# Second attention layer: reciprocals turned as 16 columns and spread to 128 rows by two DMA transfers

## The chip, the cores and the metric

One core of one Trainium2 chip runs one program. The metric is the device time of one execution in microseconds (us); smaller is better. The engines are named as the profile names them: PE is TensorE's matrix unit (PEld its weight loads), DVE is VectorE, ACT is ScalarE, POOL is GpSimd, and SP is the sync engine, which here only issues DMA transfers. The core's transfers run on 16 DMA engines.

## The reference

Two attention layers follow one another over 16 graphs of 512 tokens and 384 features (12 heads of 32). Cut to what matters here:

```python
h = maximum(layernorm(x), 0)
x = x + L0(h, adj, ...)          # scores/sqrt(32) + beta*adj, masked where adj == 0
h = maximum(layernorm(x), 0)
# L1:
scores = einsum('bqhd,bkhd->bhqk', q, k) * scale + bias      # bias = adj + adj
row_nonzero = any(scores != 0, axis=-1, keepdims=True)
p = nan_to_num(softmax(where(row_nonzero, scores, -inf)))
out = einsum('bhqk,bkhd->bqhd', p, v).reshape(b, n, h)
x = x + out @ Wo.T + bo
```

In layer 1 every row (a token of a head) of the output has to be multiplied by the reciprocal of its softmax sum, or by zero where the whole row of scores is zero. The kernel does it after the product with v and before the product with Wo.

## The kernel before

There are 32 graph passes, `g`, 16 for each layer. A pass has three chunks, `c`; a chunk is four heads (128 features). A chunk has four steps, `t`, one for each tile of 128 queries. So a pass has 12 steps, numbered 0 to 11, and the text says "step 6 of a pass". A chunk's work runs on long after its own four steps: what it does at place 14.50, counted from step 0 of its pass, falls into step 2 of the next pass.

In a step PE computes the scores of the following tile (L248). DVE adds the bias and takes the minimum (L393) and transposes the tile before in 32x32 blocks (`turn`, L406). ACT takes the four exponentials (`exp`, L516). PE also has a list of other items in each step. The table `PLACES` says where each stands: `hT` turns of the next pass's input, `qk` and `v` projections, `sums` and `zero` for the test of zero rows, `tp` turns of the chunk's last tile of probabilities, `pv` the product with v in three parts, `spread` the reciprocals, and `post` the product with Wo. All of them except `pv` write to a ring of three PSUM banks. An item may start only when the item three places ahead of it in the ring has been copied out by ACT or DVE.

Each engine runs its instructions strictly in the order of the code. On ACT, an item that PE issued in a step is normally copied in the middle of the next step's exponentials. The function `soon_of` makes an exception: everything up to the last `spread`, `tp`, `turn` or `hT` of a step's list is copied directly behind that same step's four exponentials.

SP issues `move(g, c)`, 16 transfers of 192 KB between two SBUF tensors, `pk<-pt`, in two halves of eight. The first half waits for three turned tiles of the chunk and for the `pv` of the chunk before, the second half for one more part of that `pv`. `pv` part 1 of the chunk needs the first half landed, part 2 the second. The reciprocals go this way: DVE `recip`, POOL `keep` (the mask, then a product that writes 128x512 numbers, each reciprocal repeated over the 32 columns of its head), PE `spread` (four transpositions of 128x128, L300), ACT a copy of 128x512 into `rspread`, which shares its memory with `mask` and shows under that name (L586), and DVE `scale_out` (L444), which multiplies the finished `pv` of the chunk and releases `pv_done`. `pv` part 0 of the next chunk and `post` wait for `pv_done`.

Of the kernel before, what the change touches and what calls it, by code (L numbers as in the profile page):

```python
# [6 lines left out]
F32 = mybir.dt.float32  # L7
F32R = mybir.dt.float32r
ACT = mybir.ActivationFunctionType
ALU = mybir.AluOpType  # L10
# [32 lines left out]
def chunk(s):  # L43

    return s // DT, s % DT
# [15 lines left out]
    "zero": (2.53, 6.40, 10.40),  # L61
    "tp": (3.31, 3.32, 3.33, 3.34, 7.31, 7.32, 7.33, 7.34, 11.31, 11.32, 11.33, 11.34),
    "pv": (5.20, 6.70, 8.32, 9.20, 10.70, 12.32, 13.20, 14.70, 16.32),
    "spread": (7.30, 12.30, 16.61),
    "post": (17.50, 17.60, 18.50, 20.50),
})

# [58 lines left out]
SPLITS = {(B - 1, 1, 1): 2, (B - 1, 1, 3): 0, (B - 1, 2, 1): 1}  # L126


def two_layers(nc, x, adj, weights, bq, bk, bv, bo, beta, x1, out, mem):

    scale = float(HD) ** -0.5, float(D) ** -0.5

# [6 lines left out]
    with ExitStack() as ctx:  # L139
        def sem(name):  # L140
            return ctx.enter_context(nc.semaphore(name))
# [12 lines left out]
        recip_dve, recip_done, keep_step, ksum_done = sem("recip_dve"), sem("recip_done"), sem("keep_step"), sem("ksum_done")  # L154
        v_added, biassum_done, part_done = sem("v_added"), sem("biassum_done"), sem("part_done")
        stats_done, mv_done, rstd_step, h_done = sem("stats_done"), sem("mv_done"), sem("rstd_step"), sem("h_done")
        hT_high, mask_done, bias_done = sem("hT_high"), sem("mask_done"), sem("bias_done")
        scaled, res_added, bo_added = sem("scaled"), sem("res_added"), sem("bo_added")
        last_stored = sem("last_stored")
# [5 lines left out]
        def nth(kind, g, i):  # L165
            return per_graph[kind] * (g - B if kind in ("sums", "zero", "spread") else g) + i + 1
# [17 lines left out]
        @block.sync  # L184
        def _(sp):
            def load_weight(layer, n):
                sp.dma_start(m.raw[layer][n], weights[layer][n].rearrange("(t p) n -> p t n", p=P)).then_inc(raw_in[layer][n], 16)

            def load_row(dst, row, signal):
                sp.dma_start(dst[:], row.rearrange("(a n) -> a n", a=1).to_broadcast([P, D])).then_inc(signal, 16)  # L190

            def move(g, c):

                s = DT * g + c
                if s == LAST:
                    return
                sp.wait_ge(turned, TURNS * (s + 1))
                for half in range(HALVES):
                    if s:
                        sp.wait_ge(pv_ready, PARTS * (s - 1) + half + 2)  # L200
                    for n in range(QUADS):
                        for a in (half, half + HALVES):
                            to = (a - half + n) % QUADS
                            sp.dma_start(m.pk[HD * to:HD * (to + 1), a], m.pt[HD * a:HD * (a + 1), s % 2, to]).then_inc(moved[layer_of(g)][c][half], 16)  # L204

            sp.dma_start(m.xin[:], tokens(x[0])).then_inc(x_first, 16)
            load_weight(0, 0)
            load_weight(0, 1)
            sp.dma_start(m.beta[:], beta.rearrange("(a n) -> a n", a=1).to_broadcast([P, 1])).then_inc(small_in, 16)
            sp.dma_start(m.bq[:], bq).then_inc(small_in, 16)  # L210
            sp.dma_start(m.bk[:], bk).then_inc(small_in, 16)
            load_weight(0, 2)
            load_row(m.bva, bv[0], bv_in[0])
            load_row(m.bvx, bv[1], bv_in[1])
            for g in range(GRAPHS):
                for c in range(STEPS):
                    move(g, c)

                    if (g, c) == (B - 2, 2):
                        load_weight(1, 2)  # L220
                    if (g, c) == (B - 1, 0):
                        for n, last in ((0, 2), (1, 0)):
                            sp.wait_ge(weights_split[last], 2)
                            load_weight(1, n)
                        sp.wait_ge(v_added, NT * B)
                        load_row(m.bva, bo, bo_in)
                    if (g, c) == (B, 1):
                        sp.wait_ge(res_added, NT * B)
                        sp.dma_start(m.wo[:], weights[1][3].rearrange("(t p) n -> p t n", p=P)).then_inc(wo_in, 16)
            for i in range(NT):  # L230
                sp.wait_ge(done["post"], nth("post", GRAPHS - 1, i))
                sp.dma_start(tokens(out[B - 1])[:, i], m.res[:, i, :]).then_inc(last_stored, 16)
            sp.wait_ge(last_stored, 16 * NT)

        @block.tensor
        def _(pe):
# [14 lines left out]
            def item(kind, g, i):  # L251
# [44 lines left out]
                    mm = nc.tensor.transpose(to[:, 0:P], m.headsum[:], m.ident[:])  # L296
                if kind == "spread":
                    pe.wait_ge(recip_done, nth("spread", g, i))
                    for t in range(NT):
                        mm = nc.tensor.transpose(to[:, P * t:P * (t + 1)], m.rwide[:, t, :], m.ident[:])  # L300
                if kind == "post":
                    if i == 0:
                        pe.wait_ge(pv_done, DT * (g + 1))
# [67 lines left out]
        def _(dve):  # L371
# [66 lines left out]
            def scale_out(g, c):  # L438

                if c == 0:  # L440
                    dve.wait_ge(ready["post"], nth("post", g - 1, NT - 1))
                dve.wait_ge(done["spread"], nth("spread", g, c))
                dve.wait_ge(pv_ready, PARTS * (DT * g + c + 1))
                nc.vector.tensor_tensor(m.oT[:, c, :], m.out[:], m.rspread[:], ALU.mult).then_inc(pv_done, 1)  # L444

# [63 lines left out]
        def _(act):  # L509
# [21 lines left out]
            def item(kind, g, i):  # L531
# [47 lines left out]
                    nc.scalar.activation(m.v[:, g % 2, i, :], frm[:, 0:D], ACT.Copy).then_inc(done["v"], 1)  # L579
                if kind == "spread":  # L580
                    act.wait_ge(ready["spread"], nth("spread", g, i))
                    if g == B and i == 0:
                        act.wait_ge(bias_done, NT * B)
                    else:
                        act.wait_ge(pv_done, DT * g + i)
                    nc.scalar.activation(m.rspread[:], frm, ACT.Copy).then_inc(done["spread"], 1)  # L586

            def soon_of(g, c, t):

# [42 lines left out]
        def _(pool):  # L632
# [98 lines left out]
            def keep(g, c):  # L731
# [16 lines left out]

                def wide(ap):
                    return ap.rearrange("p t (j o) -> p t j o", o=1).to_broadcast([P, NT, HC, HD])  # L750
                nc.gpsimd.tensor_tensor(m.rwide[:].rearrange("p t (j e) -> p t j e", e=HD), wide(m.recip[g % 2][:, :, HC * c:HC * (c + 1)]),
                                        wide(m.mz[:]), ALU.mult).then_inc(recip_done, 1)

# [73 lines left out]
class Memory:  # L827
    def __init__(self, nc, ctx):
        def sb(name, shape, dt=F32):
            return ctx.enter_context(nc.sbuf_tensor(name, shape, dt))  # L830
# [34 lines left out]
        self.mz, self.rz = sb("mz", [P, NT, HC]), sb("rz", [P, NT, HC])  # L865
        self.recip = [sb(f"recip{i}", [P, NT, H]) for i in range(2)]
        self.ksum1, self.ksum = sb("ksum1", [P, 2]), sb("ksum", [P, 2, HD])
        self.headsum = sb("headsum", [P, P])
        self.oT = sb("oT", [P, DT, N])
        self.onorm = self.wo  # L870
# [4 lines left out]

def two_attention_layers(nc: bass.Bass, x, adj, wq0, bq0, wk0, bk0, wv0, bv0, beta0, wq1, wk1, wv1, bv1, wo1, bo1, out):
    x1 = nc.dram_tensor("x_between", [B, N, D], F32, kind="Internal").ap()
    with ExitStack() as ctx:
        mem = Memory(nc, ctx)
        two_layers(nc, x, adj, ((wq0, wk0, wv0), (wq1, wk1, wv1, wo1)), bq0, bk0, (bv0, bv1), bo1, beta0, x1, out, mem)  # L880


# [29 lines left out]
```

## Time and profile before

| | us |
|---|---|
| median of 3 runs | 1988.66 (1985.5 to 1992.04) |
| the profiled execution | 1990.03 |
| its span | 1988.3 |
| PE busy | 1900.5 (96%) |
| DVE busy | 1828.6 (92%) |
| ACT busy | 1676.5 (84%) |
| POOL busy | 913.0 (46%) |
| mean share of the 16 DMA engines, queue of SP | 63.3% |
| the same, queue of POOL | 18.4% |

The profiled execution took 1.4 us more than the median of the runs. The span is the part of it that the trace covers. Layer 1 takes up the second half, from about 975 us on. Busy shares are averages over both layers; a share under 100% can still hide an engine that is the limit in one stage.

### The profile page before, as it was taken

The numbers are of one execution on the slowest core, as the hardware profiler recorded it, in microseconds if no ns is written. First come the engines' busy times: TensorE is split into PE (matmuls) and PEld (weight loads), VectorE is DVE, ScalarE is ACT, GpSimd is POOL, SyncE is SP. The second block draws the span as 40 slices with busy tenths as digits, with TensorE's granted clock in tenths as the row PEclk, the third lists the DMA queues.
The fourth block names the chain that finished last, engine by engine and source line by source line (L and its number), as shares of the span: only waits on it lengthen the run. The fifth ranks groups of instructions, "written<-read, shape, count | busy, mean of one in ns | idle before, by whom it ended". The sixth has DMA issues, their size and how long they took to land.

```text
span 1988.3 us, 50014 instructions
## 1 busy us (share of the span) xinstructions
PE 1900.5 (96%) x18336; PEld 1229.1 (62%) x18336; DVE 1828.6 (92%) x3989; ACT 1676.5 (84%) x4275; POOL 913.0 (46%) x1114
## 2 busy tenths in 40 slices
PE   5999999999999999997999999999999999999998
PEld 3566666666666666664666666666666666666665
DVE  5999999999999999997989999999999999999984
ACT  4999999999999999997977887887887888887885
POOL 5465556556655455561353334343343334343331
PEclk9999999999999999998999999999999999999999
DMA  3888999988899898889787788778787788777884
GB/s 134 197 215 220 228 225 234 229 228 223 230 226 230 231 233 226 226 224 225 201 218 198 187 215 222 189 202 210 193 216 194 189 221 211 199 200 202 203 200 113
DMA packets 104723, 415.92 MB, mean 209 GB/s; under 512 B 27008, under 2 KB 31104, under 8 KB 104480
## 3 DMA queue, kind: packets, MB, share of 16 engines
q1 hardware_dynamic: 77728, 305.24, 63.3%
q0 software_dynamic: 26752, 107.49, 18.4%
q8 instruction: 147, 2.41, 0.5%
q14 instruction: 96, 0.79, 0.1%
HBM read 88.61 MB, written 25.17 MB: 57 GB/s over the span
## 4 chain that ended last, share of the span: by engine, by line
PE 49%; DVE 25%; ACT 11%; DMA 6%; SPq 5%; issue 3%; POOL 1%; DVEq 0%; POOLq 0%
DVE s L393 13%; PE sc L248 11%; PE ring L281 11%; DVE pt L406 10%; PE out L340 9%; PE ring L309 6%; ACT s L516 6%; SPq L204 5%; PE ring L265 5%; PE ring L288 4%; DMA pk<-pt 4%; ACT xin L523 2%; PE ring L274 2%; ACT pl L548 1%; PE ring L300 1%
## 5 line engine op out<-in xcount | busy, mean ns | idle before, releaser
L516 ACT ACTIVATE s<-s,nmax 128x512 f32<-128x512 f32 x1536 | 1094.9, 726 | 157.6 <-DVE nmax L393 157.5
L393 DVE CUSTOM_DVE_ANT_0 s<-sc,bias 128x512 f32<-128x512 f32 x1536 | 968.0, 686 | 53.0 <-PE sc L248 25.2
L406 DVE STREAM_TRANSPOSE pt<-s 128x2048 f32<-128x2048 f32 x285 | 656.8, 2304 | 0.0
L248 PE MATMUL sc<-k,q 32*128 32x512 f32 x3072 | 439.9, 642 | 51.0 <-DVE nmax L393 36.2
L516 ACT ACTIVATION_READ_ACCUMULATOR s<-s,nmax 128x1 f32 x1536 | 311.0, 202 | 0.0
L340 PE MATMUL out<-pk,v 128*32 128x192 f32 x6080 | 287.2, 330 | 6.0 <-DMA pk<-pt 6.0
L340 PEld LDWEIGHTS out<-pk,v 128*32 128x32 f32 x6080 | 178.8, 110 | 140.4 <-issue 87.4
L288 PE MATMUL ring<-wv,hT 128*128 128x384 f32 x1152 | 236.3, 349 | 0.0
L281 PE MATMUL ring<-hT,wq 128*128 128x512 f32 x864 | 228.1, 409 | 1.5 <-DVE hT L421 1.5
L281 PE MATMUL ring<-hT,wk 128*128 128x512 f32 x864 | 228.0, 408 | 0.0
L248 PEld LDWEIGHTS sc<-k,q 32*128 32x128 f32 x3072 | 121.5, 184 | 164.0 <-DVE nmax L393 82.8
L281 PEld LDWEIGHTS ring<-hT,wk 128*128 128x128 f32 x864 | 156.3, 190 | 102.1 <-issue 72.0
L548 ACT ACTIVATE pl<-ring 128x512 f32<-128x512 f32 x384 | 198.0, 604 | 24.0 <-PE ring L265 24.0
L265 PEld LDWEIGHTS ring<-ident,s 128*128 128x128 f32 x1536 | 165.7, 141 | 77.2 <-issue 51.6
L281 PEld LDWEIGHTS ring<-hT,wq 128*128 128x128 f32 x864 | 156.4, 190 | 85.2 <-issue 52.5
L288 PEld LDWEIGHTS ring<-wv,hT 128*128 128x128 f32 x1152 | 195.7, 188 | 21.5 <-issue 17.0
L265 PE MATMUL ring<-ident,s 128*128 128x128 f32 x1536 | 196.2, 279 | 6.2 <-ACT pl L548 5.7
L686 POOL TENSOR_TENSOR v<-v,bvx 128x384 f32<-128x384 f32 x64 | 64.5, 1007 | 295.0 <-ACT v L579 295.0
L686 POOL TENSOR_TENSOR v<-v,bva 128x384 f32<-128x384 f32 x64 | 64.6, 1010 | 262.4 <-ACT v L579 262.3
L393 DVE DVE_READ_ACCUMULATOR2_ANT nmax<- 128x1 f32 x1536 | 127.5, 83 | 0.0
L309 PE MATMUL ring<-wo,oT 128*128 128x384 f32 x360 | 126.6, 495 | 0.0
L675 POOL TENSOR_SCALAR mask<-bias 128x512 f32<-128x512 f32 x64 | 123.3, 1927 | 1.3 <-DMA bias<-in_adj 0.6
(93 smaller groups left out, 1891.4 us busy)
## 6 DMA issues: line engine op xcount, KB each, us to landing
pk<-pt SPq DMA_DIRECT2D x1520, 192.0 KB, 4.9
bias<-in_adj POOLq DMA_DIRECT2D x32, 1024.0 KB, 10.3
res<-in_x POOLq DMA_DIRECT2D x16, 768.0 KB, 7.4
x_between<-res POOLq DMA_DIRECT2D x16, 768.0 KB, 4.5
xin<-x_between POOLq DMA_DIRECT2D x16, 768.0 KB, 10.1
res<-x_between POOLq DMA_DIRECT2D x16, 768.0 KB, 10.6
xin<-in_x POOLq DMA_DIRECT2D x15, 768.0 KB, 9.8
out_x<-res POOLq DMA_DIRECT2D x15, 768.0 KB, 7.0
```

The lines of the kernel that those rows point to most:

```text
L248: mm = nc.tensor.matmul(m.sc[:, j, :], m.q[rows, s % 2, P * t:P * (t + 1)], m.k[rows, s % 2, :], start=True, stop=True)
L265: mm = nc.tensor.transpose(to[:, P * n:P * (n + 1)], m.s[:, TURNS % 2, j, P * n:P * (n + 1)], m.ident[:])
L281: mm = nc.tensor.matmul(to, w[y][:, t, P * a:P * (a + 1)], m.hT[x][:, t, :], start=n == 0, stop=n == 3 * DT - 1)
L288: mm = nc.tensor.matmul(to[:, 0:D], m.hT[x][:, t, P * i:P * (i + 1)], m.wv[y][:, t, :], start=n == 0, stop=n == 3 * DT - 1)
L309: mm = nc.tensor.matmul(to[:, 0:D], o, m.wo[:, t, :], start=t == 0, stop=t == DT - 1)
L340: mm = nc.tensor.matmul(to, v[:, n, P * c + HD * j:P * c + HD * (j + 1)], p, start=n == 0, stop=n == QUADS - 1)
L393: nc.vector.tensor_tensor_reduce(out=m.s[:, t % 2, j, :], in0=m.sc[:, j, :], in1=m.bias[g % 2][:, t, :], scale=s_scale[layer], scalar=3.0e ...
L406: nc.vector.transpose(out=to, in_=m.s[:, t % 2].rearrange("p j (i a e) -> p (j i) a e", a=QUADS, e=HD)).then_inc(turned, 1)
L516: nc.scalar.activation(tile, tile, ACT.Exp, bias=m.nmax[s % 2][:, t, j:j + 1], scale=-1.0, accum_out=m.sums[s % 2][:, t, j:j + 1]).then_in ...
L548: nc.scalar.activation(m.pl[:, j, :], frm, ACT.Copy).then_inc(done["tp"], 1)
L675: nc.gpsimd.tensor_scalar(m.mask[:], tile, 0.0, masked, ALU.is_le, ALU.mult).then_inc(mask_done, 1)
L686: nc.gpsimd.tensor_tensor(v, v, (m.bva, m.bvx)[layer_of(g)][:], ALU.add).then_inc(v_added, 1)
```

## The change

Of the 48 chunks of layer 1, 47 change; the last keeps the old way. POOL now writes only 16 columns (`rcols`: four heads times four tiles). PE turns them in one transposition into 16 rows of 128. ACT copies those 16x128 numbers into `rrows`. SP then stores them to DRAM, waits until they have landed, waits for the `scale_out` of the chunk before, and loads them back, each head's row of 512 numbers repeated over 32 partitions, into `rspread`. DVE waits for that transfer instead of for ACT. The places of `spread` move from 7.30, 12.30 and 16.61 to 6.50, 10.50 and 14.50.

```diff
-    "spread": (7.30, 12.30, 16.61),
+    "spread": (6.50, 10.50, 14.50),
...
+            def spread_rows(g, c):
+
+                s = DT * g + c
+                n = s - DT * B
+                sp.wait_ge(done["spread"], nth("spread", g, c))
+                if n > 1:
+                    sp.wait_ge(spread_in, 16 * (n - 1))
+                sp.dma_start(rows[n % 2].rearrange("(r e) -> r e", e=P), m.rrows[:]).then_inc(rows_stored, 16)
+                sp.wait_ge(rows_stored, 16 * (n + 1))
+                if n:
+                    sp.wait_ge(pv_done, s)
+                else:
+                    sp.wait_ge(bias_done, NT * B)
+                sp.dma_start(m.rspread[:], rows[n % 2].rearrange("(j o n) -> j o n", j=HC, o=1).to_broadcast([HC, HD, N])).then_inc(spread_in, 16)
...
                 for c in range(STEPS):
+                    if DT * g + c > DT * B:
+                        spread_rows(*chunk(DT * g + c - 1))
                     move(g, c)
...
                     pe.wait_ge(recip_done, nth("spread", g, i))
-                    for t in range(NT):
-                        mm = nc.tensor.transpose(to[:, P * t:P * (t + 1)], m.rwide[:, t, :], m.ident[:])
+                    if DT * g + i == LAST:
+                        for t in range(NT):
+                            mm = nc.tensor.transpose(to[:, P * t:P * (t + 1)], m.rwide[:, t, :], m.ident[:])
+                    else:
+                        mm = nc.tensor.transpose(to[0:NT * HC, 0:P], m.rcols[:], m.ident[:])
...
-                dve.wait_ge(done["spread"], nth("spread", g, c))
+                if DT * g + c == LAST:
+                    dve.wait_ge(done["spread"], nth("spread", g, c))
+                else:
+                    dve.wait_ge(spread_in, 16 * nth("spread", g, c))
...
-                    if g == B and i == 0:
-                        act.wait_ge(bias_done, NT * B)
+                    if DT * g + i == LAST:
+                        act.wait_ge(pv_done, LAST)
+                        nc.scalar.activation(m.rspread[:], frm, ACT.Copy).then_inc(done["spread"], 1)
                     else:
-                        act.wait_ge(pv_done, DT * g + i)
-                    nc.scalar.activation(m.rspread[:], frm, ACT.Copy).then_inc(done["spread"], 1)
+                        if (g, i) > (B, 0):
+                            act.wait_ge(rows_stored, 16 * (nth("spread", g, i) - 1))
+                        nc.scalar.activation(m.rrows[:], frm[0:NT * HC, 0:P], ACT.Copy).then_inc(done["spread"], 1)
...
+                if s < LAST:
+                    nc.gpsimd.tensor_tensor(m.rcols[:].rearrange("p (j t) -> p t j", t=NT), m.recip[g % 2][:, :, HC * c:HC * (c + 1)],
+                                            m.mz[:], ALU.mult).then_inc(recip_done, 1)
+                    return
```

On ACT, steps 5 to 9 of a steady pass of layer 1 stood so before. L516 are exponentials, L523 the next pass's input (`xin`), L566 the copy of `k`, L586 the spread copy, L548 the copies of `tp`, L551 those of `hT`:

```order
802 L516 ACTIVATE s,sums<-s,nmax 128x512 x4
803 L523 ACTIVATE xin<-xin,nmr,rstd 128x384 x2
804 L516 ACTIVATE s,sums<-s,nmax 128x512
805 L566 ACTIVATE k,ksum<-ring 128x512
806 L516 ACTIVATE s,sums<-s,nmax 128x512 x3
807 L586 ACTIVATE mask<-ring 128x512
808 L548 ACTIVATE pl<-ring 128x512 x4
809 L551 ACTIVATE hT<-ring 128x512 x3
```

Now the same place reads (the lines of the changed file are other ones, L590 is the copy of `k`, L612 the copy of the 16 rows):

```order
793 L540 ACTIVATE s,sums<-s,nmax 128x512 x4
794 L590 ACTIVATE k,ksum<-ring 128x512
795 L612 ACTIVATE rrows<-ring 16x128
796 L547 ACTIVATE xin<-xin,nmr,rstd 128x384 x2
797 L540 ACTIVATE s,sums<-s,nmax 128x512 x4
798 L572 ACTIVATE pl<-ring 128x512 x4
799 L575 ACTIVATE hT<-ring 128x512 x3
```

The copy of `k` and the spread copy have both moved ahead of all four exponentials of step 7 and ahead of the two `xin`. The same has happened to the copy of `k` in steps 10 and 2.

On SP, one chunk of a steady pass was one `move`:

```order
245 L204 DMA pk<-pt 32x1536 [waits pv_ready,turned]
246 L204 DMA pk<-pt 32x1536 x7
247 L204 DMA pk<-pt 32x1536 [waits pv_ready]
248 L204 DMA pk<-pt 32x1536 x7
```

Now the store of the 16 rows and the load that repeats them stand ahead of it, each with waits of its own:

```order
251 L200 DMA rows<-rrows 16x128 [waits spread_in,spread_done]
252 L206 DMA mask<-rows 128x1x512 [waits pv_done,rows_stored]
253 L220 DMA pk<-pt 32x1536 [waits pv_ready,turned]
254 L220 DMA pk<-pt 32x1536 x7
255 L220 DMA pk<-pt 32x1536 [waits pv_ready]
256 L220 DMA pk<-pt 32x1536 x7
```

All 18 transfers of a chunk go through SP's one queue, and the `move` of a chunk is issued only after the store of the chunk before has landed.

## Rows read from the trace of the kernel before

**Rows 1.** Windows of one pass: busy us by engine, clock, DMA share, GB/s
```profile
1300.00:1362.00 62.00, 61.60 (x595) 39.78 (x593) 58.02 (x125) 50.13 (x133) 22.87 (x34) 1.00 0.81 204
1284.00:1286.00 2.00, 2.00 (x39) 1.21 (x41) 1.97 (x9) 2.00 (x7) 0.36 (x1) 1.00 1.04 253
```

**Rows 2.** Chain that ended last, one pass: start us, us, what
```profile
1298.58 4.07 PE ring L309 x12
...
1308.06 1.44 PE out L340 x32
...
1310.56 0.59 PE ring L300 x4
...
1314.45 1.07 PE sc L248 x8
...
1328.81 0.11 PE ring L296
...
1333.36 1.68 PE ring L288 x9
...
1336.31 0.69 DVE s L393
...
1354.50 1.14 PE sc L248 x8
1355.64 1.44 PE out L340 x32
...
1361.05 1.01 PE out L340 x32
1362.06 1.49 PE ring L309 x4
```

**Rows 3.** Groups by line in layer 1: busy us, mean ns, idle before
```profile
L586 ACT ACTIVATE mask<-ring 128x512 f32<-128x512 f32 x47 | 28.3, 601 | 32.4 <-PE ring L300 32.4
...
L576 ACT ACTIVATE headsum<-ring 128x128 f32<-128x128 f32 x46 | 12.7, 275 | 16.0 <-PE ring L293 16.0
```

**Rows 4.** Timeline, steps 6 and 7 of a pass, ACT
```profile
1302.46 1.29 ACT L523 ACTIVATE xin<-xin,nmr,rstd 128x384 f32<-128x384 f32 x2
...
1308.94 0.71 ACT L516 ACTIVATE s<-s,nmax 128x512 f32<-128x512 f32 x1
...
1311.68 2.06 ACT L548 ACTIVATE pl<-ring 128x512 f32<-128x512 f32 x4
```

**Rows 5.** Timeline, end of the last chunk
```profile
1968.66 2.08 ACT L548 ACTIVATE pl<-ring 128x512 f32<-128x512 f32 x4
...
1969.33 0.66 PE L265 MATMUL ring<-ident,s 128*128 128x128 f32 x4 [0.47 <-ACT pl L548]
```

**Rows 6.** SP's moves of a chunk, first and last: ns each, starts; landing
```profile
L204 SPq DMA_DIRECT2D pk<-pt x2: 507/552/597, 1310.9 to 1311.5; - x2
...
L204 SPq DMA_DIRECT2D pk<-pt x1: 590/590/590, 1321.9 to 1321.9; - x1
...
DMA to landing us min/median/max: 9.3/9.3/9.3
```

**Rows 7.** The same for the next chunk, first three and last two issues
```profile
L204 SPq DMA_DIRECT2D pk<-pt x3: 507/590/592, 1332.2 to 1333.4; - x3
...
L204 SPq DMA_DIRECT2D pk<-pt x2: 590/626/663, 1343.8 to 1344.5; - x2
...
DMA to landing us min/median/max: 8.4/8.7/9.1
```

**Rows 8.** DMA issues: KB each, median us to landing
```profile
out_x<-res SPq DMA_DIRECT2D x4, 192.0 KB, 1.9
...
bva<-in_bo SPq DMA_DIRECT2D x1, 192.0 KB, 4.3
```

**Rows 9.** Timeline: the product with the reciprocals in the next pass
```profile
1358.55 0.69 DVE L444 TENSOR_TENSOR oT<-out,mask 128x512 f32<-128x512 f32 x1 [0.17 <-ACT mask L586]
```

**Rows 10.** Timeline, first pass of layer 1, PE
```profile
1029.06 2.30 PE L340 MATMUL out<-pk,v 128*32 128x192 f32 x32 [2.12 <-DMA pk<-pt]
```

More of the change, by code:

```diff
@@ L126, with two_layers @@
 SPLITS = {(B - 1, 1, 1): 2, (B - 1, 1, 3): 0, (B - 1, 2, 1): 1}
-def two_layers(nc, x, adj, weights, bq, bk, bv, bo, beta, x1, out, mem):
+def two_layers(nc, x, adj, weights, bq, bk, bv, bo, beta, x1, rows, out, mem):
     scale = float(HD) ** -0.5, float(D) ** -0.5
@@ L156, in two_layers @@
         stats_done, mv_done, rstd_step, h_done = sem("stats_done"), sem("mv_done"), sem("rstd_step"), sem("h_done")
+        rows_stored, spread_in = sem("rows_stored"), sem("spread_in")
         hT_high, mask_done, bias_done = sem("hT_high"), sem("mask_done"), sem("bias_done")
@@ L867, in __init__ @@
         self.ksum1, self.ksum = sb("ksum1", [P, 2]), sb("ksum", [P, 2, HD])
+        self.rcols, self.rrows = sb("rcols", [P, NT * HC]), sb("rrows", [NT * HC, P])
         self.headsum = sb("headsum", [P, P])
@@ L877, in two_attention_layers @@
     x1 = nc.dram_tensor("x_between", [B, N, D], F32, kind="Internal").ap()
+    rows = [nc.dram_tensor(f"rows_{i}", [HC * N], F32, kind="Internal").ap() for i in range(2)]
     with ExitStack() as ctx:
         mem = Memory(nc, ctx)
-        two_layers(nc, x, adj, ((wq0, wk0, wv0), (wq1, wk1, wv1, wo1)), bq0, bk0, (bv0, bv1), bo1, beta0, x1, out, mem)
+        two_layers(nc, x, adj, ((wq0, wk0, wv0), (wq1, wk1, wv1, wo1)), bq0, bk0, (bv0, bv1), bo1, beta0, x1, rows, out, mem)
 def kernel(x, adj, L0_gnn_Wq, L0_gnn_bq, L0_gnn_Wk, L0_gnn_bk, L0_gnn_Wv, L0_gnn_bv, L0_gnn_beta,
```

## Prediction

> **What bounds the kernel now.** I read the windows first. In a steady pass of layer 1, PE is busy 61.60 of 62 us and DVE 58.02, so PE has no slack and DVE little. ACT has 50.13. The DMA engines are at 0.81 [rows 1]. The chain of waits then gives the rhythm: the two `post` products stand at 1298.58 and at 1362.06, so a pass takes 63.5 us. Most of it is PE's, except the stretch from 1336.3 to 1354.5, which is DVE's: there, PE work can go and nothing is won [rows 2]. There are 15 such intervals between the 16 passes of layer 1. Last I read SP's own moves and their landings, since the change puts two more transfers into that queue and makes SP wait for one of them.
>
> **The change part by part.**
>
> *PE.* Four transpositions are 0.59 us on the chain. A single one (the `zero` item) is 0.11 [rows 2]. In a pass, the one for chunk 2 (place 4.61, just ahead of the chain's PE part) gives back 0.59, since its successor moves to step 2, into DVE's stretch. The one for chunk 0 would give 0.48. The one for chunk 1 stood in DVE's stretch and comes back as 0.11 in step 10. Alone that is 0.96 us a pass.
>
> *ACT.* The copy shrinks from 601 ns to about the 275 ns of a 128x128 copy, and its wait for PE, 32.4 us in all, goes [rows 3]. POOL's last product shrinks too, and POOL is off the path. But ACT's order takes something back. In step 6, ACT now copies `k` and the 16 rows before `xin` and before the exponentials of step 7. PE turns the 16 columns after the `post` of that step, which ends at 1308.06 [rows 2], so they are there at 1308.2. Then come 0.28 for the copy, 1.29 for two `xin` and four exponentials of 0.71, so the copies of `tp` begin at 1312.6 and not at 1311.68 [rows 3, 4]. The four of them take 2.06 [rows 4]. The last turn of `hT` needs the fourth copy gone from the ring, so it can start at 1314.7 and ends about 0.5 later, at 1315.1. PE went on at 1314.45 before [rows 2]. So chunk 0 costs 0.65 instead of giving 0.48. That PE does wait on such a copy is seen at the end of the last chunk: the first copy starts at 1968.66, the fourth turn at 1969.33, 0.67 later, with a wait of 0.47 [rows 5]. In step 10, `k` is ready at 1328.8 [rows 2]; 0.57 for its copy, 0.28 and four times 0.71 bring the copies of `tp` to 1332.55, the fourth turn starts 0.67 later and ends by 1333.7, where PE was free at 1333.36 before [rows 2]: 0.3. In step 2 the same delay falls into DVE's stretch and costs nothing by these rows. Sum on PE and ACT: -0.59 + 0.65 + 0.3 = +0.4 us a pass.
>
> *The two transfers.* The store is small. The quickest landing of SP's is 1.9 us [rows 8]; I take that for it and 0.6 for an issue [rows 6]. The load that repeats the rows is not in the trace. From below: it writes 256 KB, and at 204 GB/s with a share of 0.81 [rows 1] that is 1.05 us of all engines. From above: the nearest row is the load of one row of `bo` to 128 partitions, 192 KB in 4.3 us [rows 8]. Less the 1.9 of a quick landing, 2.4 us by the count of its 128 rows, 3.2 by bytes. I take 2.8, as this row repeats a source too.
>
> The Trainium skill speaks to this load ("DMA: Bandwidth & Descriptors", "Why a DMA increments its semaphore by 16 and not by 1"): the number of engines is the largest up to 16 that divides the slowest dimension of both access patterns. The source's is four heads, so four engines would carry it all. No transfer in this trace has such a shape. By that rule the load costs more than its bytes suggest, and the sum would be that of the third rival below; by the bytes alone it would be that of the first.
>
> *Where these transfers stand.* SP's queue is served in order as far as the rows show: the moves of chunk 1 start at 1310.9, the last is issued at 1321.9 and lands 9.3 later, at 1331.2 [rows 6]. Those of chunk 2 start at 1332.2, the last is issued at 1344.5 and lands 9.1 later, at 1353.6 [rows 7]. PE takes that data at 1355.64 [rows 2], only 2.0 later. Now follow a pass:
> - The load for chunk 0 is issued ahead of the moves of chunk 1: they start 0.6 later and carry 2.8 more, so they end at 1334.6.
> - The 16 rows of chunk 1 are copied by ACT at about 1329.7, plus 0.65 for step 7. Their store stands behind those moves and lands at 1334.8. Before that SP issues nothing.
> - Then the load for chunk 1 (0.6) and the moves of chunk 2: from 1335.4, not 1332.2. They end at 1353.6 + 3.2 + 2.8 = 1359.6.
> - The 16 rows of chunk 2 are ready in step 2 of the next pass, around 1349, with the engines full (share 1.04 at the same place of the pass before [rows 1]). Their store lands at 1359.8. The load for chunk 2 lands 1.9 + 2.8 later, at 1364.5.
> - DVE's product with it stood at 1358.55 [rows 9]. It now ends at 1365.2. `pv` part 0 (1361.05 before) and `post` wait for it: 1.01 and 4.07 later [rows 2] PE is at 1370.3, where it was at 1366.1. That is +4.2 us a pass.
>
> A second count, by the load of the queue: 0.81 of 63.5 is 51.4 us. Three loads of 2.8 and three round trips of 2.5 (1.9 and 0.6), in which SP's queue is empty, make 67.3: +3.8 a pass. I take 4.0. The ACT term is inside the wait then, not beside it. 15 passes: +60. The first pass of layer 1 starts with PE waiting 2.12 us for a move [rows 10], and a store and a load now stand ahead of that move: +3. At the end one spread (0.6 on PE, 0.6 on ACT) leaves the chain: -1. Against the profiled execution of 1990.0 this is 2052; its distance to the median, 1.4, makes it **2050**.
>
> **The rivals.**
> - *The queue hides it.* If the load costs no more than 1.05, the same walk ends with the last load at 1359.9, and DVE's product ends by 1360.6, before PE wants it at 1361.05. The price decides from about 1.2 us on, and each us above it costs three. Then only PE and ACT count: 15 x 0.4, +3, -1: 1997. For it: the engines stand idle at times (0.81). Against it: the row of `bo`.
> - *Faster.* The transfers hide and ACT keeps up, for instance since the exponentials before run ahead of what I reckon: 15 x -0.96, -1, with nothing at the start: 1973. It is one mechanism, the ring's copies: if the copies of `tp` still begin by 1311.7, PE keeps its 0.96. For it, ACT has 12 us of slack a pass. Against it, the order on ACT, which puts 4.4 us of work between the 16 rows and those copies.
> - *Few engines carry the load.* The bytes of one DMA engine set the price: 252 GB/s in 16 parts is 15.8 GB/s, and 64 KB on each of four engines take 4.2 us. The walk then gives 4.2 + 3 x 1.4 = 8.4 a pass and the queue count 8.0: 2050 + 15 x 4.2 = 2113. The rule named above would have it so. Against it in the rows: the row of `bo` at 4.3 in all.
> - *The change moves nothing that counts*, gains and losses cancelling: 1989.
>
> **How the numbers follow.** A measurement of this kernel tells 0.3%, 6 us, from no change. Chances: the queue walk 0.56 (its own range 2015 to 2085), few engines 0.13, hidden queue 0.15, faster 0.09, nothing 0.07. The hidden queue ends 8 us above the median; 0.09 of it counts as slower and 0.06 as same. So slower 0.78, same 0.13, faster 0.09. The range leaves out the faster case and the upper part of the few engines: 1993 to 2105.
>
> **What would show it.** In the profile after: the product with `oT` (L444's successor) waiting for a DMA instead of ACT, some us, once a pass; PE `out<-pk` or `out<-pl` waiting behind it; the store of 16 rows with a landing of 5 to 10 us, not 2, in chunks 1 and 2; SP's moves of chunk 2 starting over 3 us later against the turn; PE busy share falling below 96% although its work fell by 47 x 3 transpositions. If the stores land in 2 us everywhere and the loads in 3, the walk is wrong. If the copies of `tp` are not late, the ACT term is.

## The result and the profile after

The changed kernel takes **2125.11 us** (median of 4 runs, 2106.79 to 2127.28), the kernel before 1989.87 in the same comparison (1985.5 to 1992.04). The ratio is 1.066, with an interval of 1.0634 to 1.0687: 135 us slower. The forecast was slower, at 2050, with a range up to 2105: the direction was right, the size was not, and the time lies 12 us above the third rival ("few engines carry the load", 2113).

The page of the changed kernel: busy times, the chain that ended last by engine, and three lines of the DMA issues (KB each, median us from issue to landing).

```profile
PE 1936.5 (91%) x18195; PEld 1235.4 (58%) x18195; DVE 1830.4 (86%) x3989; ACT 1653.2 (78%) x4275; POOL 874.9 (41%) x1114
...
PE 45%; DVE 17%; DMA 14%; ACT 13%; issue 5%; SPq 3%; POOL 3%; DVEq 0%; POOLq 0%
...
pk<-pt SPq DMA_DIRECT2D x1520, 192.0 KB, 5.8
...
mask<-rows SPq DMA_DIRECT2D x47, 256.0 KB
```

PE has 141 matmuls fewer than before (18195 against 18336) and is still busy 36 us longer (1936.5 against 1900.5). So time is lost in two ways: PE stands, and what it does takes longer. `mask<-rows` is the load that repeats the rows (the trace calls the region of `rspread` by the name `mask`).

The windows of two passes of layer 1, and of five short stretches inside the first of them (columns as in [rows 1]):

```profile
1320.00:1322.00 2.00, 1.08 (x32) 0.81 (x32) 1.99 (x2) 0.00 (x0) 0.00 (x0) 0.94 1.04 216
1322.00:1324.00 2.00, 0.00 (x0) 0.00 (x0) 1.97 (x4) 0.31 (x1) 0.00 (x0) 0.50 0.95 214
1326.00:1328.00 2.00, 2.00 (x9) 0.49 (x6) 1.90 (x2) 1.10 (x4) 0.00 (x0) 0.50 0.99 219
1330.00:1332.00 2.00, 2.00 (x7) 1.21 (x5) 0.67 (x3) 0.19 (x1) 0.00 (x0) 0.50 0.27 89
1332.00:1334.00 2.00, 2.00 (x37) 1.25 (x40) 1.73 (x2) 2.00 (x8) 0.36 (x1) 1.00 0.17 56
1300.00:1362.00 62.00, 55.05 (x482) 34.56 (x482) 50.49 (x113) 42.68 (x115) 19.70 (x31) 0.92 0.79 185
1362.00:1424.00 62.00, 55.48 (x506) 34.57 (x507) 50.04 (x110) 42.35 (x116) 21.32 (x36) 0.94 0.86 198
```

Before, PE was busy 61.60 of 62 us at a clock of 1.00. Now it is 55.05, and the clock is 0.92: from 1322 to 1332 TensorE runs at 0.50, its lower level of 1.2 GHz, and such a stretch, mostly of 6.8 us, comes once a pass. What it did before the fall is in the rows: it had nothing to do from 1321 on. It is the same work at half the rate that makes the busy time longer.

The waits of the changed kernel in layer 1 (1000 to 2110): who waited for what, us in total, times, longest.

```profile
DVE oT L468 <- DMA mask<-rows: 97.6, 29, 7.1
...
PE sc L266 <- DVE nmax L414: 62.6, 30, 3.7
...
PE out L361 <- DVE oT L468: 20.0, 13, 5.0
...
PE out L361 <- DMA pk<-pt: 7.6, 11, 1.5
```

The product with the reciprocals, which waited 0.17 for ACT's copy in [rows 9], now waits for the load in 29 cases, 97.6 us in all. While DVE stands there, its next item, the maxima of the scores, is late, and PE's score products wait for those (62.6). The chain of waits shows how a pass is made of this.

```profile
1305.02 0.16 ACT rrows L612
...
1305.19 5.50 DMA rows<-rrows
...
1310.71 9.28 DMA mask<-rows
...
1320.01 0.06 DVE oT L468
...
1320.62 2.31 DVE pt L427
...
1325.54 2.09 PE sc L266 x8
1327.63 4.14 PE ring L299 x9
...
1345.44 4.07 PE ring L330 x12
...
1355.22 1.29 ACT xin L547 x2
1356.51 2.82 ACT s L540 x8
1359.34 0.49 ACT pl L572
...
1359.87 0.66 PE ring L283 x4
...
1377.85 4.20 DMA rows<-rrows
...
1382.07 9.79 DMA mask<-rows
```

From one store to the next (1305.19, 1377.85) a pass takes 72.7 us. Over the 14 intervals between the products of `post` that the chain holds (1057.35 to 2062.08) the mean is 71.8, where before it was 63.6 (1044.38 to 1934.61). The chain no longer stays on PE: the 16 rows are copied at 1305.2, their store lands 5.50 later, the load takes 9.28 more, and only then can DVE's product start, 14.8 us after the copy. It is the product of chunk 1, 25 us ahead of the next `post`; in the trace before that product stood at 1338.76, 23 us ahead of its `post`. Behind it the eight score products take 2.09 us and nine pieces of the projections 4.14, at the clock of 0.50; at 1300.86 and 1302.00 in the same trace, at full clock, they took 1.14 and 2.31. That is 2.8 us more a pass.

### The profile page after: what moved, and what is told of

The parts are those of the page before. It is cut to its first block, busy times and chain, and to the rows that moved or that the text cites. A ratio compares the mean times of both kernels' runs of the same rounds, so it can differ in the third digit from the quotient of the medians.

```text
span 2122.7 us, 49917 instructions
## 1 busy us (share of the span) xinstructions
PE 1936.5 (91%) x18195; PEld 1235.4 (58%) x18195; DVE 1830.4 (86%) x3989; ACT 1653.2 (78%) x4275; POOL 874.9 (41%) x1114
## 3 DMA queue, kind: packets, MB, share of 16 engines
q1 hardware_dynamic: 85436, 317.95, 64.1%
## 4 chain that ended last, share of the span: by engine, by line
PE 45%; DVE 17%; DMA 14%; ACT 13%; issue 5%; SPq 3%; POOL 3%; DVEq 0%; POOLq 0%
PE ring L299 12%; PE sc L266 10%; DVE s L414 9%; PE out L361 7%; ACT s L540 7%; DVE pt L427 7%; DMA mask<-rows 6%; PE ring L330 6%; PE ring L283 4%; DMA rows<-rrows 4%; PE ring L306 3%; SPq L220 3%; DMA pk<-pt 3%; ACT xin L547 2%; PE ring L292 2%
## 5 line engine op out<-in xcount | busy, mean ns | idle before, releaser
L266 PE MATMUL sc<-k,q 32*128 32x512 f32 x3072 | 453.1, 660 | 106.0 <-DVE nmax L414 90.7
L540 ACT ACTIVATION_READ_ACCUMULATOR s<-s,nmax 128x1 f32 x1536 | 300.2, 195 | 0.0
L361 PE MATMUL out<-pk,v 128*32 128x192 f32 x6080 | 286.5, 329 | 10.5 <-DMA pk<-pt 10.4
L299 PE MATMUL ring<-hT,wk 128*128 128x512 f32 x864 | 251.0, 439 | 0.0
L299 PEld LDWEIGHTS ring<-hT,wk 128*128 128x128 f32 x864 | 172.8, 209 | 118.8 <-issue 83.4
L283 PE MATMUL ring<-ident,s 128*128 128x128 f32 x1536 | 207.9, 281 | 14.5 <-ACT pl L572 12.6
L572 ACT ACTIVATE pl<-ring 128x512 f32<-128x512 f32 x384 | 195.8, 589 | 13.8 <-PE ring L283 13.6
L468 DVE TENSOR_TENSOR oT<-out,mask 128x512 f32<-128x512 f32 x48 | 33.2, 691 | 129.9 <-DMA mask<-rows 97.6
L755 POOL TENSOR_SCALAR ksum<-headmask,ksum 128x32 f32<-128x32 f32 x48 | 17.7, 370 | 305.3 <-ACT k L590 304.5
L361 PE MATMUL out<-pl,v 128*32 128x128 f32 x3072 | 106.3, 280 | 31.5 <-DVE oT L468 20.0
```

The source lines that it names most:

```text
L266: mm = nc.tensor.matmul(m.sc[:, j, :], m.q[rows, s % 2, P * t:P * (t + 1)], m.k[rows, s % 2, :], start=True, stop=True)
L283: mm = nc.tensor.transpose(to[:, P * n:P * (n + 1)], m.s[:, TURNS % 2, j, P * n:P * (n + 1)], m.ident[:])
L299: mm = nc.tensor.matmul(to, w[y][:, t, P * a:P * (a + 1)], m.hT[x][:, t, :], start=n == 0, stop=n == 3 * DT - 1)
L361: mm = nc.tensor.matmul(to, v[:, n, P * c + HD * j:P * c + HD * (j + 1)], p, start=n == 0, stop=n == QUADS - 1)
L540: nc.scalar.activation(tile, tile, ACT.Exp, bias=m.nmax[s % 2][:, t, j:j + 1], scale=-1.0, accum_out=m.sums[s % 2][:, t, j:j + 1]).then_in ...
L572: nc.scalar.activation(m.pl[:, j, :], frm, ACT.Copy).then_inc(done["tp"], 1)
```

## The experiments

Two families. The first varies the load's shape, the second takes transfers or waits out. All were compared with the kernel before on the same chips (medians 1987.9 to 1989.7 there).

### The shape of the load

**One load in four.** Each head's row is repeated to its 32 partitions by a load of its own, the same bytes:

```
-                    sp.wait_ge(spread_in, 16 * (n - 1))
+                    sp.wait_ge(spread_in, 16 * HC * (n - 1))
...
-                sp.dma_start(m.rspread[:], rows[n % 2].rearrange("(j o n) -> j o n", j=HC, o=1).to_broadcast([HC, HD, N])).then_inc(spread_in, 16)
+                for j in range(HC):
+                    row = rows[n % 2][N * j:N * (j + 1)].rearrange("(o n) -> o n", o=1)
+                    sp.dma_start(m.rspread[HD * j:HD * (j + 1), :], row.to_broadcast([HD, N])).then_inc(spread_in, 16)
...
-                    dve.wait_ge(spread_in, 16 * nth("spread", g, c))
+                    dve.wait_ge(spread_in, 16 * HC * nth("spread", g, c))
```

> The changed kernel with its repeating load cut into four, one for each head's row, 32 partitions each; bytes, order and waits are the same, SP issues four instead of one. Theory 1 (the load is slow since its outermost dimension of four keeps it on four of the 16 engines): each piece now spreads over 16 engines, the set lands 3 to 5 us after its first issue instead of 9.3, and most of the 9.2 us a pass comes back: 2000 to 2035. Theory 2 (the load is slow because it and the store queue behind the moves, whatever its shape): the set lands as late as before, three more issues cost 1.8 us a chunk, 2115 to 2160.

Measured 2012.8 us (2009.35 to 2019.49), ratio 1.012 (1.0093 to 1.0146). 112 of the 135 us are gone with the same bytes, the same store, the same wait and three more issues. In the page and the waits of this kernel (columns as above):

```profile
mask<-rows SPq DMA_DIRECT2D x188, 64.0 KB, 2.1
...
DVE oT L470 <- DMA mask<-rows: 16.2, 11, 4.6
```

The product's waits fell from 97.6 to 16.2 us. The 2.1 is each piece from its own issue; the last of the four lands 3.8 us after the first issue in the median (3.2 to 7.3). The theory that only the number and the bytes of the transfers count falls here.

**Loads of 16 and of 8 rows.** One load as in the change, with 16 (or 8) source rows each repeated 8 (or 16) times. The rows are of `adj`, so the scaling of layer 1 is by other numbers; the store and the wait for it stay. The edit with r = 16 and r = 8:

```
-                sp.dma_start(m.rspread[:], rows[n % 2].rearrange("(j o n) -> j o n", j=HC, o=1).to_broadcast([HC, HD, N])).then_inc(spread_in, 16)
+                sp.dma_start(m.rspread[:], adj[0][0:r].rearrange("j (o n) -> j o n", o=1).to_broadcast([r, P // r, N])).then_inc(spread_in, 16)
```

> The changed kernel, still one load of 256 KB in rows of 2 KB with all waits, but the source is 16 rows of adj, each repeated 8 times, instead of 4 rows repeated 32 times. Outputs of layer 1 are scaled by other numbers. Only the outermost dimension of the source differs. Theory 1 (its size sets the number of engines): the load lands in about 3 us, and the time is that of the four loads or a little under, 2000 to 2013. If the four loads were faster for another reason than the engines, such as their smaller size: 2100 or more.

> As the one with 16 rows, but 8 rows, each repeated 16 times. Outputs of layer 1 are scaled by other numbers. Theory 1: eight engines carry 32 KB each, the load lands between the two others, about 5 to 6 us, and the time lies between: 2015 to 2070. If the shape doesn't matter: as the changed kernel, 2115 to 2130.

Measured: 16 rows 1999.79 us (1.0059, 1.0037 to 1.0082), 8 rows 2029.78 (1.0208, 1.0184 to 1.0233), beside 2125 with 4. The mean pass, from the chains as above, is 64.1, 66.2 and 71.8. So one load of 256 KB is not slow for its size: with 16 rows on the outside it does as well as the four small ones, and a little better. It has a landing in the page, 3.6 us:

```profile
mask<-in_adj SPq DMA_DIRECT2D x47, 256.0 KB, 3.6
```

That with 8 rows has none there, as the one of the change; its chain shows it, with the store ahead of it (5.4 to 7.4 us over the whole chain):

```profile
1211.22 4.94 DMA rows<-rrows
1216.18 6.22 DMA mask<-in_adj
...
1278.34 2.94 DMA rows<-rrows
1281.30 6.56 DMA mask<-in_adj
...
1482.33 5.98 DMA mask<-in_adj
```

The landing is missing in these two pages because the trace holds fewer updates of the load's semaphore by DMA engines than the 16 a transfer that the page reckons with. Their number is a finding in itself. Over the 47 loads it is 752 with 16 rows, 423 with 8 and 235 in the change: 16, 9 and 5 a load. With 8 and with 4 rows the first of them comes about 1 us after the issue (0.99 to 1.16), and the other 8 and 4 at 3.3 and 4.5 us at the earliest; with 16 rows none comes before 2.6. So I read the early one as no engine's data and each of the others as one engine's: 16, 8 and 4 engines. The four small loads have 16 each.

With the last update taken as the landing, all 47 loads can be compared, from the issue: with 16 rows 3.6 us in the median (3.4 to 6.1), with 8 rows 5.2 (4.3 to 7.7), with 4 rows 8.2 (5.5 to 10.5). The Trainium skill has such a rule ("DMA: Bandwidth & Descriptors", "Why a DMA increments its semaphore by 16 and not by 1"): the number of engines is the largest up to 16 that divides the slowest dimension of both patterns. The 16, 8 and 4 of the updates agree with it; the time does not double with each halving of that number.

### What the transfers are worth

**No transfers at all.** The store, the load and their waits are gone, DVE waits for ACT's 16-row copy alone; layer 1 is scaled by what `rspread` happens to hold. What is left of the change is its work on PE, ACT and POOL.

```
                 for c in range(STEPS):
-                    if DT * g + c > DT * B:
-                        spread_rows(*chunk(DT * g + c - 1))
                     move(g, c)
...
-                if DT * g + c == LAST:
-                    dve.wait_ge(done["spread"], nth("spread", g, c))
-                else:
-                    dve.wait_ge(spread_in, 16 * nth("spread", g, c))
+                dve.wait_ge(done["spread"], nth("spread", g, c))
```

> The changed kernel without the store and without the load: DVE waits for ACT's copy of the 16 rows and multiplies with what lies in the tile, so the outputs of layer 1 are not scaled by the reciprocals. It holds only the PE, ACT and POOL part of the change. Theory 3 (ACT's new order costs a good part of the loss): 2020 or more. My reckoning of the prediction, +0.4 us a pass less 1 at the end: 1994 to 1999. If ACT keeps up, PE's 0.96 us a pass is seen: 1972 to 1978.

Measured 1997.37 us (10 runs), ratio 1.0042 (1.0028 to 1.0056): the work itself is slower, by 8 us, though it is less. A pass takes 64.05 (the products of `post` at 1304.72 and 1368.76, for one), 0.6 more than the 63.5 of most passes before. Its chain shows why:

```profile
1378.23 0.12 PE ring L311
...
1378.55 1.29 ACT xin L534 x2
1379.84 2.83 ACT s L527 x8
1382.67 0.48 ACT pl L559
...
1383.20 0.66 PE ring L273 x4
```

PE's one transposition releases ACT's 16-row copy, behind which stand the two `xin`, the four exponentials (two entries each) and the copy of `pl`, and PE's last turn of `hT` waits for that copy.

**The places moved up, with and without transfers.** One number per chunk in the table, so that ACT copies the 16 rows ahead of `k`:

```
-    "spread": (6.50, 10.50, 14.50),
+    "spread": (6.05, 10.05, 14.05),
```

> The kernel without transfers with the earlier places. Outputs of layer 1 are not scaled. If ACT's order behind the places 6.50, 10.50 and 14.50 is what costs the 0.4 us a pass (1997 instead of 1974), this one shows the whole gain on PE: 1970 to 1980. If it is something else in the smaller work or in the ring, it stays at 1990 to 1998.

> The changed kernel with the places of spread at 6.05, 10.05 and 14.05 instead of 6.50, 10.50 and 14.50: the 16 columns are turned before the k projection of their step, so ACT no longer copies k ahead of the exponentials and the 16 rows are ready 2.3 us or more earlier. The load stays on four engines. If the chain through store and load sets the rhythm, each pass gets about 3 us shorter: 2070 to 2090. If the engines' throughput on the four loaded ones sets it, the earlier start gives little: 2110 to 2125.

Without transfers: 1975.82 us, ratio 0.9929 (0.9909 to 0.9949), 22 us below the same kernel with the places of the change. A pass takes 62.6, 0.9 below before, and PE's `ring` no longer stands behind `pl` (waits of 0.5 in all against 7.0). With the transfers of the change: 2106.92 (1.0584, 1.056 to 1.0607), 18 us better than the change, and between the two cases expected (up to 2090, from 2110). The product still waits 104.5 us for the load. So the order on ACT is a term of its own, some 20 us, and not the cause of the 135.

**One load, or four, that nobody waits for.** To the kernel without transfers a load (or four) of rows of `adj` is added ahead of each chunk's moves, into a region that DVE doesn't read. It waits for nothing but its own predecessor.

```
+                if n:
+                    sp.wait_ge(extra_in, 16 * n)
...
+                sp.dma_start(to, adj[0][0:HC].rearrange("j (o n) -> j o n", o=1).to_broadcast([HC, HD, N])).then_inc(extra_in, 16)
```

> The kernel without transfers plus one repeating load a chunk at the place in SP's queue where the change has it, four rows of adj to 128 partitions of a tile that nobody reads; no store, no round trip, DVE does not wait for it. Outputs of layer 1 are not scaled. Theory 1: the load lands 6 us or more after its issue, and the moves behind it end later: 10 to 60 us above the kernel without transfers. Theory 2: it lands in about 3 us and costs under 6 us in all.

> As the kernel with one load alone, but the load in four pieces of one row and 32 partitions each. Outputs of layer 1 are not scaled. Theory 1: 16 engines carry each piece, the landings are near 3 us, and the time is within 10 us of the kernel without transfers although SP issues three more. Theory 2: no better than the one load.

Measured: one load 2006.0 us (1.0083), four loads 1997.6 (1.0041), without any 1997.4. Four loads of these bytes cost nothing that can be measured: the engines have room for them. The one load costs 8.6 us in all, between the two cases expected (under 6, from 10). PE waits for moves four times in layer 1, 12.1 us together, the longest 9.8:

```profile
PE out L362 <- DMA pk<-pt: 12.1, 4, 9.8
```

Of the 14 passes of the chain 12 take 64.0 to 64.1, as without transfers, one takes 64.3 and one 67.7; the first `post` is 2.9 us later. Yet these loads are slow, 12.3 us from issue to landing in the median (7.8 to 19.8), and have 5 updates each as in the change. So the load's shape does its harm through who waits for its landing, and only to a small part by the room that it takes from the moves.

**No round trip.** The load takes rows of `adj` (again the scaling is by other numbers) in the change's shape, and SP does not wait for the store:

```
-                sp.wait_ge(rows_stored, 16 * (n + 1))
...
-                sp.dma_start(m.rspread[:], rows[n % 2].rearrange("(j o n) -> j o n", j=HC, o=1).to_broadcast([HC, HD, N])).then_inc(spread_in, 16)
+                sp.dma_start(m.rspread[:], adj[0][0:HC].rearrange("j (o n) -> j o n", o=1).to_broadcast([HC, HD, N])).then_inc(spread_in, 16)
```

> The changed kernel with SP not waiting for the store's landing; the one load (four engines) reads four rows of adj, so that nothing depends on the store. Outputs of layer 1 are not scaled. If store's wait and the load add up on one chain (5.5 and 9.3 us in the trace), taking the wait away gives back 3 to 5.5 us a pass: 2045 to 2080. If the load on four engines alone is the cause, 2100 or more.

A miss: 2006.88 us (1.009, 1.0066 to 1.0113), although the load is the four-row one. Its passes take 64.05, as without transfers. What it has above that kernel is at the start of layer 1, in one wait on its chain:

```profile
1022.26 11.27 DMA mask<-in_adj
...
1058.63 1.49 PE ring L329 x4
```

The first `post` stands at 1058.63, 10 us later than without transfers (1048.51). So the four-row load fits when it need not wait for the store. But it is not the load of the change with the store's time taken away: it is shorter itself. In the 14 chunks 1 from the second on it lands 5.5 us after its issue in the median (5.4 to 6.1), against 8.9 in the change (6.7 to 10.5). Two windows, each from issue to landing of one load of chunk 1 (columns as in [rows 1]), first without the wait for the store, then in the change:

```profile
1282.91:1288.64 5.73, 5.69 (x49) 3.89 (x45) 5.49 (x12) 5.73 (x17) 3.34 (x5) 1.00 0.53 137
```

```profile
1310.71:1319.99 9.28, 7.99 (x75) 4.96 (x74) 3.54 (x11) 5.83 (x17) 3.87 (x8) 1.00 0.92 213
```

Without the wait the engines have a share of 0.53 during the load, and the next move 2.1 us behind it. With the wait it stands at a share of 0.92, the next move 0.7 us behind it. In chunk 2 of the kernel without the wait the share during the load is 0.90 on the mean, and the load, of rows of `adj`, takes 9.0; so it is not the source that makes it slow. The share goes with the length; how far the moves cause it was not varied by itself.

### Is there a better version?

**Four loads and the early places.**

> Both repairs, outputs as the reference: four loads of one head each and the earlier places. By my sums the transfers are hidden and ACT's order costs nothing, so that PE's 0.96 us a pass is left over: 1973 to 1985. If the round trip of the store still stands on the chain, 1990 to 2010.

Measured 2002.44 us (1.0072, 1.0046 to 1.0098): not the first case but the second, 27 us above the same places without transfers. On the chain of the profiled execution (1997.68, the shortest of the four) some passes take 62.6, others 63 to 70, 64.2 on the mean, and the longest waits of SP's queue are now for its own store:

```profile
SPq L208 <- DMA rows<-rrows: 290.0, 46, 8.7
```

**The store issued by ACT.** As the last one, but ACT issues the store behind its copy, and SP only waits for it:

```
+                        n = nth("spread", g, i) - 1
+                        act.wait_ge(done["spread"], n + 1)
+                        if n > 1:
+                            act.wait_ge(spread_in, 16 * HC * (n - 1))
+                        act.dma_start(rows[n % 2].rearrange("(r e) -> r e", e=P), m.rrows[:]).then_inc(rows_stored, 16)
```

> The kernel with both repairs (four loads, places 6.05, 10.05, 14.05), and ACT issues the store itself right after its copy, in a queue of its own, while SP only waits for the landing. Outputs as the reference. If what is left of the loss (2002 against 1976 without transfers) is the store queueing behind SP's moves, most of it goes: 1976 to 1990. If it is the traffic, or SP being held back from the next moves, it stays at 1995 to 2010; ACT's own waits can cost up to 0.5 us a chunk.

Measured **1984.31 us** (9 runs, 1980.56 to 1987.77), ratio 0.9974 (0.9964 to 0.9984): 141 us below the change and 5 below before. The interval lies below 1, but by less than the 0.3% that counts here. A pass takes 62.9 on the mean. The timeline of SP and ACT shows what the store gained; first the kernel with SP's store, then that with ACT's (start us, us, engine, line, tiles):

```profile
1338.33 11.44 SPq L222 DMA_DIRECT2D pk<-pt  x16
1349.87 0.52 SPq L200 DMA_DIRECT2D rows<-rrows  x1
1357.50 1.71 SPq L208 DMA_DIRECT2D mask<-rows  x4
```

```profile
1333.83 11.18 SPq L218 DMA_DIRECT2D pk<-pt  x16
...
1346.29 0.31 ACTq L615 DMA_DIRECT2D rows<-rrows  x1
...
1354.01 1.70 SPq L204 DMA_DIRECT2D mask<-rows  x4
```

SP can issue the store of chunk 2 only when it has issued all 16 moves, at 1349.87. ACT issues it at 1346.29, right behind its copy (1346.01), and the loads start at 1354.01 in place of 1357.50. The way from the issue to the load did not get shorter (7.6 with SP, 7.7 with ACT; the store's median landing is 6.9 from ACT's queue). It is the issue that comes earlier. Over 14 passes, chunk 2's four loads have landed 12.4 us after ACT's copy on the mean with SP's store and 11.0 with ACT's, chunk 0's 14.4 and 10.7. Without transfers the two products stand 12.3 and 14.4 behind the copy. So chunk 0 gains more than chunk 2, and the total wait of SP for the store (290 us in the view above) is no measure of the loss.

**The kernel before with chunk 2's spread early.** The one gain that the change has by its places alone, `"spread": (7.30, 12.30, 14.50)` in the kernel before:

> The kernel before with one number changed: the spread of chunk 2 at place 14.50 instead of 16.61, so four transpositions move from PE's stretch of the chain into the stretch that is DVE's. If the chain is read rightly, a pass gets up to 0.59 us shorter, less what PE's small slack in DVE's stretch does not cover: 1980 to 1985. If PE is the limit everywhere in the pass, nothing changes: 1988 to 1991.

Measured 1986.71 us (11 runs), ratio 0.9984 (0.9974 to 0.9993), 63.28 a pass, 0.21 less than the 63.49 of most passes before. By the medians that is 2.2 us, by the ratio 3, a third of what 0.59 a pass would give (9), and between the two cases expected (up to 1985, from 1988). Its interval too is below 1 by less than 0.3%.

## Why the prediction came out as it did

**What held.** *PE alone* was priced at -0.96 us a pass; without transfers and with ACT out of the way a pass is 62.61 against 63.49: -0.88. *ACT's order* was to take that back and leave +0.4; measured is +0.56, and the chain of the kernel without transfers has the very instructions in it, though at step 7 only. The times follow: the "hidden" rival's 1997 is what the kernel without transfers takes (1997.4), the "faster" rival's 1973 is near that with ACT's order mended (1975.8). Part of the first agreement is luck: the 1997 has +3 at the start of layer 1 for the transfers, and the kernel without them has +4.1 there (first `post` at 1048.51, before 1044.38). *The store* was to have "a landing of 5 to 10 us, not 2" in chunks 1 and 2. Over the 14 passes of the chain it is 4.9 in the median for chunk 1 (2.3 to 6.1), the low end of that, and 3.2 for chunk 2. In the pass shown, chunk 2's takes 2.2 (issued at 1332.67, the load behind it at 1334.92), when the stall had let the queue run empty (a share of 0.17 in the last short window).

**The step that failed: "I take 2.8" for the load.** It was taken between 1.05 and 3.2, on top of a quick landing of 1.9, from a load of one row to 128 partitions. So the walk let this load land 4.7 us after its issue. It has four rows on the outside and lands 8.2 us after it in the median, 8.9 in chunk 1. A row with a different outermost dimension was no price for it. The rival of few engines named the mechanism, and its price (4.2, so a landing of 6.1) too was below what was measured. That its 2113 is near the 2125 is in good part luck: it comes of the walk's "three times" the price, at chunk 2, and the time is lost in another way and at another chunk.

**With it, the hinge was wrong.** The walk ended at chunk 2's product. On the chain it is chunk 1's that waits, in 13 of the 14 passes. The trace before has that product in the timeline of DVE:

```profile
1338.76 0.69 DVE L444 TENSOR_TENSOR oT<-out,mask 128x512 f32<-128x512 f32 x1
```

With the 16 rows at 1329.7, as the prediction reckoned them, the room is 9.1 us. In the kernels where nothing holds it up, the product stands 9.4 behind the copy, and chunk 2's 9.7. I had the load for chunk 1 in the walk, but did not hold it against this row. By the count used for chunk 2 (a store landed at 1334.8, then 1.9 and 2.8) it lands at 1339.5, already 0.7 late. Measured, it lands 13.6 us after the copy on the mean, 4.2 late. Each experiment that kept the wait or the load can be set against that room. All figures are us, means over 14 chunks 1 and 14 chunks 2, those of the 14 passes of the chain:

| kernel | chunk 1: copy to landing | product over 9.4 | chunk 2: product over 9.7 | mean pass over 64.05 |
|---|---|---|---|---|
| four rows, no wait for the store | 5.9 | 0.0 | 0.2 | 0.0 |
| 16 rows | 5.7 | 0.1 | 0.1 | 0.1 |
| four loads | 8.3 | 0.1 | 0.9 | 0.8 |
| 8 rows | 9.6 | 1.0 | 1.7 | 2.2 |
| the change | 13.6 | 4.3 | 1.7 | 7.7 |

(With 16 rows the load of one chunk 1 took 6.1 behind a store of 4.1, and DVE waited 0.85 for it, which PE did not feel.) The order of the kernels is that of their delays. In the first four lines the two delays together come near the loss of the pass. The last line has more: chunk 1's 4.3 is on the chain, chunk 2's mostly not, and 3.4 are left. The prediction had no term for most of it: the clock. While PE stands in this pass the granted clock falls to 0.50, and the next score products and projections cost 2.8 more. Of the remaining 0.6, 0.4 may be the last of these passes, where chunk 2's product is 6.1 late.

**The queue walk failed as well, in the other direction.** By it a load at 2.8, landing after 4.7, costs +4.2 a pass, and each us less takes 3 us off that. The load with 16 rows lands after 3.6, which is 1.7 in these terms, and the walk still gives about +1; that kernel costs nothing beside the ACT term (64.1 a pass against 64.05). With 8 rows (5.2, so 3.3) it gives +5.7 where 2.2 was measured. The step behind this is "they end at 1353.6 + 3.2 + 2.8 = 1359.6": the late start and the load were added in full to the end of chunk 2's moves. In the 16-row kernel the last of these moves is issued at 1348.9 and lands 9.9 later, the store issued at 1353.61 lands 5.4 later, and the load 3.5 after that. With the 4.6 us by which that trace runs behind the one before, the moves end at 1354.2 and the store lands at 1354.4, against 1359.6 and 1359.8 in the walk, and the product of chunk 2 waits for nothing. The share of 0.81 said that there was room. The second count used it, but added the round trips as time in which nothing else moves. So 2050 was partly two errors against each other: a load landing after 4.7 and not 8 us, in a queue that I took for full. A slip in the rival of the hidden queue: by the walk's own count its last load lands at 1359.3 and not 1359.9, so the bound on the price is 1.4 and not 1.2.

**The sum.** The pass: +8.2 measured, +4.0 forecast. The 14 intervals give 115 of the 134 us between the two spans (2122.7 and 1988.3). The start of layer 1 has +13 (first `post` at 1057.35, before 1044.38) where +3 was forecast: about 4 of them are there without transfers too, its first product of chunk 1 waits for a load of 8.67 on the chain, and the clock falls there for 10.2 us (3.4 before). The last 7 are in the stretch after the last `post` on the chain (60.6 against 53.7), a part of a pass and the end.

**What stays open.** Four loads with the early places have irregular passes and 27 us more than the kernel without transfers; the store from ACT takes back 18 of them. That kernel's loads land earlier behind the copy, above all in chunk 0; a second queue and an SP that is free meanwhile came with it and were not separated. The four-row load takes some 5.5 us at a share of about half; what lengthens it to 8 and 10 in the change was seen beside a share of 0.9 and the moves right behind it, and not tested by itself.

## To carry over

Look at the outermost dimension of both sides of each repeated DMA before its bytes, and cut a broadcast load by rows when it is small: here four one-row loads of 64 KB have all landed 3.8 us after the first issue in the median, where one of 256 KB with four rows takes 8.2. A round trip through DRAM is priced against the room between its producer and its consumer in each chunk; what exceeds that room is paid, and again in clock if TensorE stands for it. When an item moves in a hand-written order, list what the next engine has between its copy and the copy that the first one waits for: a place 0.45 earlier was worth some 20 us here.

## What the runs showed of the hardware, unexpected

- A load's landing hung on the outermost dimension of its pattern, at the same bytes and in the same queue: 3.6 us in the median with 16, 5.2 with 8, 8.2 with 4. DMA engines updated its semaphore 16, 9 and 5 times a load.
- The same four-row load took 5.4 to 6.1 us where the engines' share was about half, and 6.7 to 10.5 at the change's place, at a share of 0.92 on the mean.
- A slow load that nobody waits for (12.3 us to its landing in the median) cost 8.6 us in 47 issues and not 47 times its length; four quick ones cost nothing measurable (1997.6 against 1997.4).
- A store of 8 KB lands 4.2 us after its issue in the median in SP's queue (least 1.3, most 7.4), and 6.9 in ACT's: its size says nothing about its landing while 192 KB moves are under way.
- When PE stood for lack of scores, from about 1321, the granted clock was 0.94 in the row of 1320 to 1322, 0.50 in those up to 1332 and 1.00 after; at 0.50, nine pieces of the projections took 4.14 us in place of 2.31.
